# Two attention layers on one core: layer 0's input channel-major from the host, two elementwise steps of layer 1 on GpSimd, a new item order

## The reference

```python
# layer 0, 8 heads of 64: softmax of q over a head's channels, of k over the tokens
xn = ln(x, ln_w, ln_b)
q = softmax_head(xn @ Wq + bq);  k = softmax_tokens(xn @ Wk + bk + (1 - mask) * -1e6)
v = (xn @ Wv + bv) * mask
att = k^T v per head;  y = q @ att
scale, shift = split(silu(cond) @ W_emb + b_emb)
x = x + silu(ln(y, ln2_w, ln2_b) * (1 + scale) + shift) @ W_out + b_out
# layer 1, 16 heads of 32: softmax attention over 512 x 512 scores per head
xn = ln(x); q, k, v = projections of xn, v * mask
y = softmax(q k^T + (1 - mask of the key) * -1e6, over the keys) @ v
x = x + silu(ln(y) * (1 + scale) + shift) @ out_w + out_b
```

## Time and profile before

| what | value |
|---|---|
| runs | 1352.27, 1351.97, 1345.44 us; median 1351.97 |
| profiled execution | 1352.28 us |
| its span, first to last instruction | 1350.5 us |
| mean granted TensorE clock | 0.967 |
| PE / DVE / ACT / POOL busy | 97% / 70% / 72% / 26% of the span |
| layer 0, a steady batch | 58.02 us |
| layer 1, a steady batch | about 101 us |
| DMA | 173.76 MB, mean 129 GB/s |

### The profile page before, as it was taken

How to read it: one execution, slowest core, us unless ns; L and a number is a source line. 1 busy time by engine, 2 the same in 40 slices (tenths; PEclk the granted TensorE clock), 3 DMA queues, 4 the chain that set the end, 5 groups by cost and what they waited for, 6 DMA issues and landing times.

```text
span 1350.5 us, 25321 instructions
## 1 busy us (share of the span) xinstructions
PE 1311.5 (97%) x9592; PEld 1048.4 (78%) x9592; DVE 950.1 (70%) x1930; ACT 966.7 (72%) x2147; POOL 345.2 (26%) x367
## 2 busy tenths in 40 slices
PE   8999999999999999899999999999999999999998
PEld 5788888888888876577787787787787787786666
DVE  5756766666676766666876876876876876877556
ACT  5444344354434548788998998999999999998884
POOL 0323234432334460100500501501501501400302
PEclk9999999999999999899999899899899899899879
DMA  9111111211112356755455455555555545554512
GB/s 336 49 40 63 40 63 62 80 63 40 63 40 87 110 180 190 218 173 158 152 163 158 153 162 158 163 152 158 165 150 158 175 141 157 170 145 126 161 37 87
DMA packets 83994, 173.76 MB, mean 129 GB/s; under 512 B 7304, under 2 KB 8328, under 8 KB 83872
## 3 DMA queue, kind: packets, MB, share of 16 engines
q1 hardware_dynamic: 83872, 172.14, 41.1%
HBM read 104.45 MB, written 67.14 MB: 127 GB/s over the span
## 4 chain that ended last, share of the span: by engine, by line
PE 75%; ACT 12%; DVE 6%; POOL 3%; issue 2%; DMA 1%; SPq 0%; DVEq 0%; POOLq 0%; ACTq 0%
PE ps L526 15%; PE ps L528 14%; PE ps L527 14%; PE ps L705 9%; ACT ps L872 7%; PE ps L521 6%; PE ps L679 6%; PE ps L687 6%; ACT Pb L882 3%; PE ps L630 2%; PE ps L612 2%; POOL yb L1293 1%; DVE st L984 1%; DVE cT L1120 1%; PE ps L540 1%
## 5 line engine op out<-in xcount | busy, mean ns | idle before, releaser
L872 ACT ACTIVATE ps<-ps,cT 128x512 f32<-128x512 f32 x512 | 352.4, 769 | 22.9 <-DVE cT L1120 22.9
L1120 DVE TENSOR_REDUCE cT<-ps 128x1 f32<-128x512 f32 x512 | 321.6, 682 | 66.1 <-PE ps L679 65.8
L882 ACT ACTIVATE Pb<-ps 128x512 f32<-128x512 f32 x512 | 271.3, 669 | 38.4 <-PE ps L687 37.8
L679 PE MATMUL ps<-Ks,Qs 98*128 98x512 f32 x512 | 198.6, 449 | 18.2 <-ACT ps L872 14.7
L679 PEld LDWEIGHTS ps<-Ks,Qs 98*128 98x128 f32 x512 | 100.2, 198 | 80.2 <-ACT ps L872 49.1
L687 PE MATMUL ps<-Qs,Ks 100*128 100x512 f32 x512 | 158.9, 407 | 2.9 <-DVE sg_q L1111 1.2
L872 ACT ACTIVATION_READ_ACCUMULATOR ps<-ps,cT 128x1 f32 x512 | 161.5, 315 | 0.0
L1293 POOL TENSOR_TENSOR yb<-yb,cU 128x512 f32<-128x512 f32 x14 | 20.6, 1486 | 428.0 <-DVE cU L1166 428.0
L687 PEld LDWEIGHTS ps<-Qs,Ks 100*128 100x128 f32 x512 | 95.6, 189 | 38.2 <-ACT Pb L882 11.3
L526 PE MATMUL ps<-xTh,Wh_k 128*128 128x512 f32 x256 | 108.6, 424 | 5.5 <-DVE Wl_k L922 2.9
L1217 POOL TENSOR_TENSOR rs<-ve,mhalf 128x4 f32<-128x4 f32 x32 | 33.0, 1031 | 286.3 <-DVE ve L969 222.8
(11 more groups left out here) (159 smaller groups left out, 2718.0 us busy)
## 6 DMA issues: line engine op xcount, KB each, us to landing
Qs<-stack_scratch SPq DMA_DIRECT2D x32, 768.0 KB
Ks<-stack_scratch SPq DMA_DIRECT2D x32, 768.0 KB
stack_scratch<-sg_q SPq DMA_DIRECT2D x32, 512.0 KB, 2.7
stack_scratch<-sg_k SPq DMA_DIRECT2D x32, 512.0 KB, 2.6
wr<-in_x SPq DMA_DIRECT2D x32, 256.0 KB, 5.0
x_scratch<-wr SPq DMA_DIRECT2D x32, 256.0 KB, 2.0
stack_scratch<-sg_q SPq DMA_DIRECT2D x32, 256.0 KB, 2.9
stack_scratch<-sg_k SPq DMA_DIRECT2D x32, 256.0 KB, 2.9
```

Source lines behind the costliest of these rows:

```text
L679: e.matmul(bank[:], Qs[par][0:RX, j, t * 128:(t + 1) * 128], Ks[par][0:RX, j, :], start=True, stop=True).then_inc(s["S"], 1)
L872: e.activation(bank[:], bank[:], ACT.Exp, bias=nx[:, n % 2, j, t, 0:1], accum_out=dn[:, b % 2, t, 4 * g + j:4 * g + j + 1]).then_inc(s["S_ ...
L882: e.activation(Pb[m][:, j, :], ps[bank_of["a", n, m, j]][:], ACT.Exp).then_inc(s["P"], 1)
L1120: e.tensor_reduce(nx[:, n % 2, j, t, 0:1], ps[bank_of["S", n, j, t]][:], AX.X, ALU.max, negate=True).then_inc(s["S_max"], 1)
```

## The change

1. **x of layer 0, batches 1 to 7.** The host gives a second copy of x, xT0, with channels on the partitions. xr (8 KB a partition) holds a batch of it. The statistics still come from xin. POOL writes them into lnc, DVE transposes lnc to lnT (four 32 x 32 transposes), SP stores 8 rows of it to a DRAM scratch and loads that back to all partitions (rn). New item xn, in q's stage: POOL multiplies each chunk of xr with 1/sigma and adds -mean/sigma (two operations with full tiles). tx of these batches: DVE applies ln_w and ln_b in place (one tensor-scalar), ACT rounds into xTh, DVE writes the difference to xTl. PE, the PSUM bank, one ACT step and POOL's four scalings of xin fall away. SP waits for xTl of a batch, not for its transposes, before it loads the next x and xT0.
2. **Layer 1, x = 9 to 15:** the bias add of V writes to SBUF, which gives the bank back, and POOL multiplies with the mask in place. **x = 8 to 14:** POOL, not ACT, rounds y's silu to sTh, ahead of its remainder.
3. **First loads:** We0 (4 MB) and bo0 move behind x and xT0 of batch 1; Wq follows Wv. The condition products m and mb move from k's and v's stages of batch 0 to q's and o's; nx(1) moves from the end of v's stage to its beginning.
4. **All positions in `PLAN` are new.** Two for example:

```diff
-    "0o": ((1.083, 1.166), (0.409, 1.001), (0.43, 0.514)),
+    "0o": ((0.38, 0.95), (0.253, 0.703), (0.272, 0.718)),
+    "0n": ((0.023, 0.64),),
```

```diff
             def tx(i, x, c):
-                if i == 0:
+                if i == 0 and not turned_on_host(x):
                     bank = take(("tx", x, c))
...
+                    if turned_on_host(x):
+                        e.wait_ge(s["x_f"], 4 * (x - 1) + c + 1)
+                        e.copy(xTh[:, c, :], xr[:, c, :]).then_inc(s["xT_hi"], 1)
+                        return
...
-                if i == 5:
+                if i == 5 and x <= 8:
...
+                    if not in_bank(x):
+                        return
...
+                if i == 5 and turned_on_host(x):
+                    e.wait_ge(s["x_nr"], x + 1)
+                    if x > 1:
+                        e.wait_ge(s["l_ln0"], 16 * (x - 1))
+                    for u in range(4):
+                        r = e.transpose(lnT[:, 32 * u:32 * u + 32], lnc[32 * u:32 * u + 32, :])
+                    r.then_inc(s["x_T"], 1)
...
+                if i == 0 and turned_on_host(x):
+                    p = cols[0]
+                    e.wait_ge(s["xn"], 4 * x + c + 1)
+                    e.tensor_scalar(xr[:, c, :], xr[:, c, :], p[:, c:c + 1], p[:, 4 + c:5 + c],
+                                    ALU.mult, ALU.add).then_inc(s["x_f"], 1)
+                if i == 1 and turned_on_host(x):
+                    e.wait_ge(s["xT_hi"], 4 * x + c + 1)
+                    e.tensor_tensor(xTl[:, c, :], xr[:, c, :], xTh[:, c, :].bitcast(F32), ALU.subtract).then_inc(s["xT_lo"], 1)
+                    return
...
-                    e.tensor_tensor(ps[bank_of["v", x, t]][:], ps[bank_of["v", x, t]][:], bvB[:], ALU.add).then_inc(s["v_add"], 1)
+                    dst = ps[bank_of["v", x, t]][:] if x <= 8 else xbuf(x)[:, t, :]
+                    e.tensor_tensor(dst, ps[bank_of["v", x, t]][:], bvB[:], ALU.add).then_inc(s["v_add"], 1)
...
+            def xn(i, x):
+                if i == 0:
+                    e.wait_ge(s["l_ln1"], 16 * x)
+                    e.wait_ge(s["l_xT"], 16 * x)
+                e.tensor_tensor(xr[:, i, :], xr[:, i, :], rn[:, 0, :], ALU.mult).then_inc(s["x_m"], 1)
+                e.wait_ge(s["x_m"], 4 * (x - 1) + i + 1)
+                e.tensor_tensor(xr[:, i, :], xr[:, i, :], rn[:, 1, :], ALU.add).then_inc(s["xn"], 1)
+
+            def v(i, x, t):
+                if i == 5 and x > 8:
+                    e.wait_ge(s["v_add"], 4 * x + t + 1)
+                    row = xbuf(x)[:, t, :]
+                    e.tensor_scalar(row, row, mk[:, x % 8, t:t + 1], None, ALU.mult).then_inc(s["v_hi"], 1)
...
+                        e.wait_ge(s["y_s"], 4 * x + c + 1)
+                        e.tensor_scalar(t4(sTh[:, c, :]), yb[:, :, c * 128:(c + 1) * 128], 1.0, None, ALU.mult).then_inc(s["s_hi"], 1)
...
             def tx(i, x, c):
                 if i == 1 and c == 3 and x < 7:
-                    e.wait_ge(s["tx"], 4 * x + 4)
+                    if x == 0:
+                        e.wait_ge(s["tx"], 4)
+                    else:
+                        e.wait_ge(s["x_st"], 4 * x + 4)
+                        e.wait_ge(s["xT_lo"], 4 * x + 4)
                     load_x(x + 1)
+                    e.dma_start(xr[:], A["xT0"][x + 1]).then_inc(s["l_xT"], 16)
+                    if x == 0:
+                        load_we()
+
+            def nx_(i, x):
+                if i == 6 and turned_on_host(x):
+                    e.wait_ge(s["x_T"], x)
+                    e.dma_start(lnd.rearrange("a (t n) -> (a t) n", t=NT), lnT[0:8, :]).then_inc(s["l_ln0"], 16)
+                    e.wait_ge(s["l_ln0"], 16 * x)
+                    if x > 1:
+                        e.wait_ge(s["xn"], 4 * x)
+                    e.dma_start(rn[:], lnd.partition_broadcast(128)).then_inc(s["l_ln1"], 16)
```

More of the change, by code:

```diff
@@ L53 @@
[L53 to L57, removed]
@@ new lines @@
+    "zq": ((0.291, 0.367, 0.624), (0.054, 0.287, 0.363), (0.326, 0.436, 0.68), (0.157, 0.979, 1.082)),
+    "zk": ((0.36, 0.512, 0.661), (0.106, 0.651, 0.652), (0.002, 0.278, 0.857), (0, 0.143, 0.512)),
+    "zstack": ((1.089, 1.2), (0.821, 1.09), (0.733, 1.118), (0.107, 0.598)),
+    "tle": (None, None, None, (0.652, 1.092)),
+    "zz": ((0.568, 0.955), (0.66, 1.048), (0.977, 1.058), (1.053, 1.189)),
+    "lr": ((0.022, 0.741), None, None, None),
+    "1v": ((0.338, 1.05), (0.128, 0.574), (0.112, 0.35)),
@@ L141, in the_order @@
               ([("ty", b - 1, c) for c in range(5)] if past else [], *PLAN["0q"][1]),
-              ([("mb", 0, 1)] if first else [], 0.1, 0.75),
+              (first_m[0] if first else [], *PLAN["f"][3]), ([("mb", 0, 0)] if first else [], *PLAN["f"][4]),
+              ([] if last else [("xn", b + 1)], *PLAN["0n"][0]),
               (wpart(1, "v") if last else [], *PLAN["1v"][1]))
@@ L228, in bank_uses @@
         return [p] if i == 0 else [], [p] if i == 5 else []
+    if k == "tx" and turned_on_host(p[1]):
+        return [], []
     if k in ("tx", "te") or (k == "ty" and p[2] < NC and not in_bank(p[1])):
@@ L369, in cond_two_layers @@
         qrc = sb("qrc", [128, 2, H0], c=c0)
+        rn = sb("rn", [128, 2, T], c=c0)
+        lnc = sb("lnc", [128, 32], c=c0)
+        lnT = sb("lnT", [32, 128], c=c0)
         c0.close()
@@ L794, in v @@
                         if t == 0:
-                            e.wait_ge(s["tx"], 4 * x + 4)
-                        if x == 8 and t == 0:
+                            e.wait_ge(s["tx"], tx_count(x, 3))
                             e.wait_ge(s["l_mk"], 32)
@@ L1071, in y @@
                     g -= 1
-                    if b and g == 0:
-                        e.wait_ge(s["yn_tr"], 4 * b)
+                    if g == 0:
+                        e.wait_ge(*((s["yn_tr"], 4 * b) if b else (s["em"], 4)))
                     e.wait_ge(s["y_mm"], 4 * b + g + 1)
@@ L1222, in nx_ @@
             def nx_(i, x):
+                if i == 4 and turned_on_host(x):
+                    e.wait_ge(s["x_ve"], x + 1)
+                    if x > 1:
+                        e.wait_ge(s["x_T"], x - 1)
+                    else:
+                        e.wait_ge(s["ln_set"], 1)
+                    e.tensor_tensor(lnc[:, 0:4], ve[:, 0, :], mhalf[:], ALU.pow).then_inc(s["x_rs"], 1)
+                    e.wait_ge(s["x_nm"], x + 1)
+                    e.wait_ge(s["x_rs"], x + 1)
+                    e.tensor_tensor(lnc[:, 4:8], nm[:, 0, :], lnc[:, 0:4], ALU.mult).then_inc(s["x_nr"], 1)
+                    return
                 if i == 4:
                     scales("x", 0, x)
-                if i > 4 and x:
+                if i > 4 and x >= 8:
                     t = i - 5
@@ L1296, in _ @@
             prologue()
-            parts = {"nx": nx_, "ny": ny, "q": q, "qn": qn, "o": o, "ty": ty, "ones": ones, "tlx": tlx}
+            parts = {"nx": nx_, "xn": xn, "ny": ny, "v": v, "q": q, "qn": qn, "o": o, "ty": ty, "ones": ones, "tlx": tlx}
             for p, i in order:
@@ L1344, in prologue, with load_we @@
                 e.dma_start(mk[:], A["mk"]).then_inc(s["l_mk"], 16)
[L1345 to L1352 removed]
+                load_w("q")
+                e.dma_start(bqB[:], A["bq0"].partition_broadcast(128)).then_inc(s["l_bq"], 16)
+            def load_we():
+                for r in range(4):
+                    src = A["We0"][512 * (r % 2):512 * (r % 2) + 512, 512 * (r // 2):512 * (r // 2) + 512]
+                    e.dma_start(e_home(r), src.rearrange("(k p) d -> p k d", p=128)).then_inc(s[f"l_we{r}"], 16)
                 e.dma_start(boB[:], A["bo0"].partition_broadcast(128)).then_inc(s["l_bo"], 16)
@@ L1483, in _ @@
             prologue()
-            parts = {"w": w, "m": m, "tx": tx, "k": k, "ty": ty, "o": o, "ahead": ahead, "stacks": stacks, "narrow": narrow, "qk": qk,
+            parts = {"w": w, "m": m, "nx": nx_, "tx": tx, "k": k, "ty": ty, "o": o, "ahead": ahead, "stacks": stacks, "narrow": narrow, "qk": qk,
                      "stack": stack, "nxt": nxt, "lx": lx, "lr": lr, "end": end}
```

89 lines of the change are left out of this document (46 added, 43 removed), and 18 rows, old and new, of tables (COST, PLAN).

## The result

The changed kernel takes **1330.87 us** (median of 4 runs, 1326.22 to 1333.63), the kernel before beside it 1351.56 (1345.44 to 1352.27): ratio 0.9847, 95% interval 0.9822 to 0.9872. Its profiled execution took 1329.64 us, span 1327.8, so it stands against the 1352.28 and 1350.5 of the earlier trace rows. The kernel before was run again beside each set of experiments, with medians of 1351.56 (beside the changed kernel), 1349.72, 1351.53 and 1349.40: medians of different sets can be compared to some 2 us, and the ratio to the kernel before is the safer measure.

The account below looks back on a forecast made before the run. PE was taken to bound the kernel (busy 97% of the span), with an ACT-bound 25.0 us in each layer 1 batch. Terms -12.25 + 6.0 + 0 - 4 - 1.5 = -11.75 gave 1340.3 us, range 1325 to 1357.

Parts of the forecast that it names:

- Transposes, -12.25: Layer 0, batches 1 to 7: PE loses 16 xin transposes between q and o products, 1.75 us a batch, -12.25 us.
- Fourth xTl chunk late, +6.0: Layer 0, before the k products: chunk 3 of xTl 1.0 us late in batches 2 to 7, +6.0 us.
- Q: End of a layer 0 batch's last q product, after which the new xTh chain starts; chunk 3 due about Q + 12.9.
- four meetings at 0.4 us: DVE's xTl chain in layer 0: four of eight operations lengthened beside POOL, 0.4 us each, +1.6 us a batch.
- Batch 0 to 1, "0 in both": Layer 0, batch 0 to 1: cover stays near 6.5 us, chunk 3 at about Q + 12 in both kernels, 0.
- First loads, 0, bounds -2 and +2: Start: x of batch 1 ahead of We, the mask_scratch transfer landing later; 0 taken, between -2 and +2 us.
- POOL, DVE and SP in layer 0, 0: Layer 0: POOL's normalization, DVE's scalings and small transposes, SP's extra transfers cost PE's path nothing, 0.
- Layer 1, -4: Layer 1: ACT's relief by moving roundings and V copies to POOL, 0.7 us a batch in six, -4 us.
- the order elsewhere, -1.5: New positions at the change of layers, last batch and end: 1.5 us gain, bounds -8 and +8.
- In the other 80.7 us PE is full: Layer 1 batch outside the 25.0 us ACT-bound part: PE never without work, so most of ACT's relief becomes idle time.
- The first rival: All is gained: -12.25 stands, layer 1 boundaries 1.5 us shorter each (-9), order -3: 1328 us; chance 0.20.

Follow-up runs that it names:

- e8: Changed kernel with the scaling of xr in layer 0 on ACT (two activations a chunk) instead of on DVE: 1318.82 us.
- e11: Changed kernel with the 4 MB of We loaded ahead of x of batch 1 instead of behind it: 1338.18 us.
- e1: Changed kernel with the old order from the change of layers on (32 PLAN entries set back), layer 0's kept: 1349.86 us.
- e5: Changed kernel with the old order from the change of layers on and both layer 1 moves to POOL undone, leaving layer 0's part: 1343.26 us.
- e6: Changed kernel with the old order from the change of layers on and POOL's V mask and y rounding written as two operations: 1340.44 us.
- e3: Changed kernel with V's mask and the rounding of y back on ACT in layer 1, new order and layer 0 kept: 1349.19 us.
- e12: Changed kernel with only the rounding of y back on ACT in layer 1, V's mask staying on POOL: 1330.93 us.
- e7: Changed kernel with POOL's V mask and y rounding written as two operations in one instruction, values unchanged: 1326.54 us.
- e4: Kernel before with the new order from the change of layers on (32 PLAN entries), no moves and no layer 0 part: 1355.32 us.
- e10: Changed kernel with DVE's scaling of chunks 0 and 1 issued earlier, in the q stage: 1322.40 us.
- e9: Changed kernel with both the xr scaling on ACT in layer 0 and POOL's two-operation form in layer 1: 1318.64 us.

## Why the prediction was right in sign and range, and off by 9 us

The time lies in the range and on the side forecast, 9.4 us under the 1340.3. The range was 32 us wide and took in no change as well, so that the time lies in it says little. The gain was 20.7 us by the medians where 11.75 had been forecast. By its terms, in the order of the prediction:

- **Transposes, -12.25: right in kind, 12% too high.** e8, where the replacement is on time, has a period of 56.46 instead of 58.02: 1.56 a batch, not the 1.75 of the chain's row.
- **Fourth xTl chunk late, +6.0: right in sum, by a different way.** Worked out was Q + 13.9; in the batch around 172 us the last subtraction ended at 185.74, Q (counted as in the prediction, 171.69 + 0.40) being 172.09: Q + 13.7. From the first k product of batch 2 to that of layer 1 the kernel before takes 352.0 us, the changed one 350.0, e8 343.5: 6.5 us of lateness, 6 x 1.0 forecast. Two things differed. My four meetings at 0.4 us were priced by the subtraction; in this batch two scalings, which I had put at 0.54 us, took 1.24 and 1.27 beside POOL and two subtractions 1.01 instead of 0.64: two meetings of 0.7 and two of 0.4. And the lateness is uneven: against e8's periods of 56.46 four of the six intervals lose 0.6 to 0.9 us, the last 0.9, but the one from the first k product of batch 6 to that of batch 7 loses 3.0 (59.42 us), with longer meetings and a wait outside the forecast's 0.5 to 1.5:

```profile
349.06 1.55 DVE L1039 TENSOR_TENSOR xTl<-xr,xTh 128x512 fp32r<-128x512 f32 x1
350.54 1.51 DVE L1035 TENSOR_SCALAR xr<-xr,cols 128x512 f32<-128x512 f32 x1
...
356.51 0.50 PE L544 MATMUL ps<-xTh,Wh_k 128*128 128x512 f32 x1 [0.74 <-DVE xTl L1039]
359.62 0.50 PE L544 MATMUL ps<-xTh,Wh_k 128*128 128x512 f32 x1 [1.71 <-DVE xTl L1039]
```

By the rule of the Trainium skill, SBUF — State Buffer, section "SBUF: two separate sides", the chain came to Q + 14.6; the trace agrees that both sides are lengthened, and ends it 0.9 us earlier.
- **Batch 0 to 1, "0 in both": wrong by 1.4 us, and by 3.5 in this trace.** From the first k product of batch 1 to that of batch 2 1.75 us less had been forecast. The eight other traces take 0.3 less in the median (61.2 against 61.54), this one 1.8 more (63.33). The step that failed is "chunk 3 comes at about Q + 12": three of four scalings took 1.27 to 1.32 us, and PE waited 3.0 us in three instead of 1.4 in two. The fall of the clock comes on top in some executions.
- **First loads, 0, bounds -2 and +2: held in sum, for a reason that I had not seen.** Batch 1's first k product comes 3.1 us earlier (62.43 against 65.56); 1.75 of that had been forecast for its transposes, which leaves 1.4. But with We first the same kernel is 7.3 us slower (e11): the new place of nx(1) needs the new order of the loads. I had looked at the mask (ACT waited 6.5 us for it instead of 2.9, without harm) and not at what stands behind the statistics on DVE.
- **POOL, DVE and SP in layer 0, 0: held.** POOL's chunk 3 stood ahead of two of its softmax subtractions, which ran from 173.26 on, but ACT's first rounding (176.68) then waited for DVE's scaling and not for the exponentials behind them.
- **Layer 1, -4, and the order elsewhere, -1.5: here is most of the miss.** Two steps failed. First, the price: I took L1230's 0.77 us (two operations) for POOL's single ones; they took 1.56 and 1.49. The chain of sTh, for which I had 12.1 us and some 2.2 to spare (769.5 against 769.2 + 2.5), takes 15.1 in e1 (from 751.9 to 767.0), and PE waits 0.8 to 1.9 us for it in each batch. With the old order this turned my -4 into +6.6 (e5 to e1), and e6 turns it back. Second, "In the other 80.7 us PE is full", from which I took ACT's relief to be idle time: true of the old order, not of the new, in which V's mask on ACT holds the scores up ahead of a PV product (e3, with V's mask on POOL again e12). The steady batches gained 0.7 us each (3.4 in five), which is the size forecast; whether by the forecast's reason, V's banks given back sooner, no run shows (e6 against e5, the moves in the two-operation form with the old order, has 1.0 in five). I had added the two terms as if each could be priced with the other left out. The runs give a square: with layer 0's part done, neither 1343.3 (e5), moves alone 1349.9 (e1), order alone 1349.2 (e3), both 1330.9. Each alone costs 6, both gain 12. With POOL's two-operation form the square is 1343.3 (e5), 1340.4 (e6), 1349.2 (e3), 1326.5 (e7): the moves no longer cost anything by themselves, but the two still don't add. My bounds for the order, -8 to +8, took in the order alone (e4: +5.6), not the 19 us that it is worth on top of the moves.

Sum by the medians: -8.3 for layer 0's part (forecast -6.25, but a good part of what was measured lies behind layer 0), -12.4 for moves and order (forecast -5.5), together -20.7. The first rival (1328) came nearest to the time, with a false ground: it asked for xTl on time, and layer 0 gained 3.4 us of its 12.25. By place the forecast was worse than its total: layer 0 brought 3.4 us where 6.25 were forecast, and what lies behind it 19.3 (by the two traces) where 5.5 were. That the one miss hides a part of the other is luck. The time that layer 0 did not bring is shown by e8 and e10: turned into waits, in some executions into a slower clock besides, and to be had by a shorter series. The version with the scaling on ACT (e8, 1318.8 us) beats both kernels, by 2.4% and 0.9%.

## What to carry to other kernels

A written-out order and the costs that it orders are one thing: price them together, and test the square (neither, each, both), since one half of a good pair can look like a loss. When a transpose or another PE step is replaced by a chain on other engines, count the operations in series behind the last reader of the buffer, at the durations that they have beside a busy neighbour; what does not depend on that reader is issued ahead of it. Give an instruction the duration of a row only if that row has the same form, down to the number of operations.

## What the runs showed that I had not expected

- POOL's tensor-scalar of 128x512 f32 with one operation takes 1.56 us, with two (the second adds 0.0) 0.696; writing the rounded type 1.494 and 0.622 (changed kernel and e6). The two operations instead of one were worth 9.4 us with the old order, 4.3 with the new one, and nothing once the scaling was on ACT (e9 against e8).
- DVE's tensor-scalar from SBUF to SBUF takes 0.533 us at least and mostly 1.24 to 1.32 beside POOL (thirteen of 28; the longest 1.51). Its subtraction with two SBUF inputs takes 0.64 when it starts first, even if POOL's product starts 0.2 us later (182.21 and 182.38 us), and 1.01 when it starts inside a POOL addition (179.92, the addition having begun at 178.91); the longest took 1.55.
- With the scaling on ACT the layer 0 batches last 56.46 us five times running, in spite of subtractions of 1.00 and 1.15 us on DVE in each of them: once the series has slack, the meetings cost nothing.
- With the same layer 0 and the same three waits of PE (1.53, 0.95 and 0.94 us) the clock stayed full between batch 0 and 1 in e6 and fell for some 3 us in e7. One trace of each kernel is not enough to price a fall of the clock.
